# Two-layer decoder on one core: weights fetched one stage ahead, expert sends one to a step, routing in groups of two

## The reference, cut to what matters

```python
x = _layernorm(x + _L0_attn_ref(x, W_Q, b_Q, W_K, b_K, W_V, b_V, W_O, b_O))      # stage a
x = _layernorm(x + _L0_xattn_ref(x, ctx_1024, ...))                              # stage b
x = _layernorm(x + _L0_ffn_ref(x, router_w, e_bias, W_gate, W_up, W_down,
                               shared_gate, shared_up, shared_down))             # cd, m, cc
x = _layernorm(x + _L1_attn_ref(x, weight_qkv, weight_out))                      # stage d
x = _layernorm(x + _L1_xattn_ref(x, ctx_1024, Wq, Wk, Wv, Wo, gq, gk))           # stage e
x = _layernorm(x + _L1_ffn_ref(x, gate_w, gate_proj, up_proj, down_proj))        # r, n, fc
```

```python
G = jnp.einsum('ecd,edi->eci', Xp, W_gate); U = jnp.einsum('ecd,edi->eci', Xp, W_up)
Y = jnp.einsum('eci,eid->ecd', jax.nn.silu(G) * U, W_down)
out = jnp.zeros((T, d), x.dtype).at[slots_token].add(Yf)
shared = jax.nn.silu(x @ shared_gate.T) * (x @ shared_up.T) @ shared_down.T
```

## Time and profile before

| | us |
|---|---|
| median of 3 runs | 3529.71 (3528.15 to 3530.47) |
| the profiled execution | 3531.17 |
| its span | 3529.2 |

### The profile page before, as it was taken

How to read it: one execution, slowest core, us unless ns; L and a number is a source line. 1 busy time by engine, 2 the same in 40 slices (tenths; PEclk the granted TensorE clock), 3 DMA queues, 4 the chain that set the end, 5 groups by cost and what they waited for, 6 DMA issues and landing times. The chain is left out here.

```text
span 3529.2 us, 59019 instructions
## 1 busy us (share of the span) xinstructions
PE 3179.0 (90%) x21140; PEld 2651.9 (75%) x21140; DVE 2078.1 (59%) x3732; ACT 1277.4 (36%) x3276; POOL 1443.5 (41%) x1470
## 2 busy tenths in 40 slices
PE   6999999999969999799896999599999999759992
PEld 5887878878847777677685777488888888748881
DVE  4666566676646666421164777466666678335566
ACT  2333333333346666201102333244444444224340
POOL 3454343444322434300162222355555566344445
PEclk9999999999979999889898999799999999679996
DMA  4001016023210100349663111411101000156664
GB/s 167 20 17 50 0 35 229 0 93 114 90 68 29 54 26 20 143 137 343 195 151 104 37 44 35 144 35 32 35 23 35 12 23 12 55 206 220 220 222 155
DMA packets 138293, 320.20 MB, mean 91 GB/s; under 512 B 18473, under 2 KB 30505, under 8 KB 135586
## 3 DMA queue, kind: packets, MB, share of 16 engines
q1 hardware_dynamic: 121058, 280.90, 23.5%
q0 software_dynamic: 15360, 36.25, 3.9%
q10 hardware_dynamic: 1728, 1.07, 0.1%
HBM read 234.21 MB, written 98.04 MB: 94 GB/s over the span
## 5 line engine op out<-in xcount | busy, mean ns | idle before, releaser
L377 POOL TENSOR_TENSOR a_sq<-a_tq,a_sinq 128x256 f32<-128x256 f32 x128 | 149.8, 1190 | 355.6 <-DVE a_tq L448 355.6
L377 POOL TENSOR_TENSOR a_sk<-a_tk,a_sink 128x256 f32<-128x256 f32 x128 | 123.7, 985 | 90.0 <-DVE a_tk L448 90.0
L343 ACT COPY a_probT<-bank 128x512 f32<-128x512 f32 x64 | 37.5, 585 | 327.5 <-PE bank L653 327.5
L390 POOL TENSOR_TENSOR e_sk<-e_tk 128x512 f32<-128x512 f32 x64 | 66.7, 1042 | 210.3 <-DVE e_tk L475 210.3
L330 ACT ACTIVATE a_sm<-a_sm,a_nmax 128x128 f32<-128x128 f32 x256 | 99.8, 391 | 121.4 <-DVE a_nmax L535 121.4
L335 ACT ACTIVATE e_prob<-bank,e_nb,e_rq 128x128 f32<-128x128 f32 x256 | 113.7, 455 | 82.5 <-DVE e_nb L540 82.5
L881 ACT ACTIVATE b_prob<-bank,b_nb 128x128 f32<-128x128 f32 x512 | 139.0, 386 | 10.0 <-DVE b_nb L1077 10.0
L975 POOL TENSOR_TENSOR d_prob<-d_prob,d_nmax 128x1024 f32<-128x1024 f32 x32 | 64.0, 1999 | 181.7 <-DVE d_nmax L1072 181.7
L2203 POOL TENSOR_TENSOR n_wu_lo<-nw_wu,n_wu_hi 128x1408 fp32r<-128x1408 f32 x23 | 74.1, 3223 | 143.4 <-DVE n_wu_hi L2247 143.4
L470 DVE TENSOR_TENSOR a_kr<-a_kr,a_sk 128x512 f32<-128x512 f32 x64 | 66.4, 1038 | 88.9 <-POOL a_sk L377 88.9
L1074 DVE TENSOR_REDUCE b_nmax<-bank 128x8 f32<-128x1024 f32 x64 | 77.7, 1214 | 67.4 <-PE bank L1213 66.7
(11 more groups left out here) (507 smaller groups left out, 10669.1 us busy)
## 6 DMA issues: line engine op xcount, KB each, us to landing
packed<-all_zero SPq DMA_DIRECT2D x32, 1024.0 KB, 8.0
cw_wg<-in_c_wg SPq DMA_DIRECT2D x32, 512.0 KB
cw_wu<-in_c_wu SPq DMA_DIRECT2D x32, 512.0 KB
cw_wd<-in_c_wd SPq DMA_DIRECT2D x32, 512.0 KB
nw_wg<-in_f_wg SPq DMA_DIRECT2D x23, 704.0 KB
nw_wu<-in_f_wu SPq DMA_DIRECT2D x23, 704.0 KB
nw_wd<-in_f_wd SPq DMA_DIRECT2D x23, 512.0 KB
n_xe<-packed SPq DMA_DIRECT2D x46, 256.0 KB, 2.7
```

Of the source, the lines that this page charges most:

```text
L343: nc.scalar.copy(probT[:], pP[:, :]).then_inc(act_pt, 1)
L377: step = nc.gpsimd.tensor_tensor(o, i, s, ALU.mult)
L390: nc.gpsimd.tensor_tensor(sk[:], tk[:], tk[:], ALU.mult).then_inc(g_k, 1)
```

## The change

There are five edits.

1. One buffer `staged` of three parts holds the raw weights for all stages and lives as long as the kernel; `first_x` holds the first x tile of a stage. Stage a's first weights (q, k, v) and its first x tile are fetched in the opening block, behind the identity and before and after the two small constants. Each stage then fetches the next one's ahead: a fetches b's x tile and q, k, v, o (on SP, in the slot of group 3, batch 14, after a wait until its own weights have been split and all but its last stores have landed); b fetches the shared expert's three weights (on SP, before the last four stores), and cd and cc both use these, so both loads `part.load` go; cc fetches d's q, k and v (on ACT, each after the last use of the part it replaces); d fetches e's v, k, q (on SP). The first x tiles of d and e, and d's wo, are still loaded in their own stage. The load of the second x tile no longer waits for the first tile to be turned.
2. In `PLAN_8` the eight sends of a pair lie one to a step: four in steps 4 to 7 of the odd slot, four in steps 0 to 3 of the next even one. The last four of pair 5 go to the beginning of POOL's queue in cd. The pieces of the output move: ("o2", 8, 10) goes behind "p" in step 0, and the output of steps 6 and 7 is cut at 4, 6, 8.
3. The experts' buffers `xe` and `ye` of stage m lie in parts of `base` that are free then.
4. In cc the last batch adds its four gathered rows to x first, and the output of the shared expert last.
5. In r there are eight groups of two batches, each counted after the first batch of the next group. SP's queue in r ends with a wait for all sends and then the loads of stage n's first x tiles, which stood in stage n.

```diff
-            sp.dma_start(xin[:], x_src[0]).then_inc(x_in, 16)
+            if not head_ready:
+                head.fetch(sp)
+            sp.dma_start(xin[:], x_src[1]).then_inc(x_in, 16)
             context(0, 0)
-            for n in QK:
-                weights(n, 0)
             biases(0)
-            weights("v", 0)
-            sp.wait_ge(pe_x, done(0))
-            sp.dma_start(xin[:], x_src[1]).then_inc(x_in, 16)
             context(1, 1)
...
+                if ahead and g == G - 1 and is_batch(b, B - 2):
+                    for n in "kvo":
+                        sp.wait_ge(w_lo[n], rows_of[n] * G)
+                    if keep is None:
+                        sp.wait_ge(out_st, 16 * (B - 4))
+                    ahead(sp)
...
-            for n in KINDS:
-                sp.dma_start(raw[n][:], w_dram["w" + n]).then_inc(w_in[n], 16)
+            if "o" not in staged.raw:
+                sp.dma_start(raw["o"], w_dram["wo"]).then_inc(w_in["o"], 16)
             sp.dma_start(xres[:], x_src(0)).then_inc(r_in, 16)
...
+            if ahead:
+                for n in KINDS:
+                    sp.wait_ge(w_lo[n], 1)
+                ahead(sp)
             for b in range(B - 4, B):
...
-                    if isinstance(e, int) and b % 2 and b >= 5:
-                        router.send(pool, b // 2 - 2, e)
+                    if isinstance(e, int) and (b % 2, e >= 4) in ((1, False), (0, True)) and b >= 5:
+                        router.send(pool, (b - 1) // 2 - 2, e)
...
-        ["x", ("o2", 8, 10), "s", "p", ("o2", 10, 12)],
+        ["x", "s", "p", ("o2", 8, 12)],
...
-        ["s", "p", ("o", 0, 2), 1, ("o", 2, 5), 2],
-        ["p", ("o", 5, 7), 3, ("o", 7, 8), "pv"],
+        ["s", "p", ("o", 0, 2), 1, ("o", 2, 4), 2],
+        ["p", ("o", 4, 6), 3, ("o", 6, 8), "pv"],
...
-    "pool": [["c"], [], ["n"], ["q"], [0, 1], ["zl", "k", 2], [3, 4, 5], [6, 7]],
+    "pool": [["c", 4], [5], ["n", 6], ["q", 7], [0], ["zl", "k", 1], [2], [3]],
...
-            part.load(sp)
             prefetch(sp)
 
         @block.gpsimd
         def _(pool):
+            for n in range(router.K, 2 * router.K):
+                router.send(pool, LAST - 2, n)
...
-    GROUPS = ((0, 2), (2, 2), (4, 4), (8, 4), (12, 4))
+    GROUPS = [(b, 2) for b in range(0, B, 2)]
...
                 weights.load(sp, weights.number(sp, 0, w), w)
+            sp.wait_ge(sent, 16 * K * B)
+            for w in range(2):
+                weights.load_x(sp, packed.rearrange("(t r) d -> t r d", r=P), weights.place(sp, 0, w), w)
...
-                if g and b == GROUPS[g][0] + 1:
+                if g and b == GROUPS[g][0]:
                     count(g - 1)
...
+                for n, used in (("q", part.pe_g), ("k", part.pe_u), ("v", part.pe_o)):
+                    act.wait_ge(used, done(part.COUNT - 1))
+                    ahead(act, n)
...
-            if shared:
-                part.load(sp)
...
+                if shared_last:
+                    dve.wait_ge(part.pe_o, done(b - part.first))
+                    dve.wait_ge(v_k, done((K - 1) * b + K - 1))
+                    nc.vector.tensor_tensor(acc[:, n], part.pO[:, :], acc[:, n], ALU.add).then_inc(v_acc, 1)
...
                 sp.dma_start(ident[:], c["ident"]).then_inc(c_in, 16)
+                head_a.fetch(sp)
                 sp.dma_start(tri[:], c["tri"]).then_inc(c_in, 16)
                 sp.dma_start(ones[:], c["ones"]).then_inc(c_in, 16)
+                for n, source in first_of(of("a_")):
+                    staged_a.fetch(sp, n, source)
                 sp.wait_ge(g_z, 1)
                 sp.wait_ge(c_in, 48)
```

More of the change, by code:

```diff
@@ L782, in _ @@
             sp.sem_inc(out_st, 16)
-            sp.dma_start(xin[:], x_src(0)).then_inc(x_in, 16)
+            if not head_ready:
+                head.fetch(sp)
             if router:
@@ L1156, in turn_x @@
             def turn_x(b):
-                pe.wait_ge(x_in, landed(b))
+                first = isinstance(b, int) and b == 0
+                t = head.tile if first else xin
+                if first:
+                    pe.wait_ge(head.x_in, 16)
+                else:
+                    pe.wait_ge(x_in, landed(b - 1))
                 pe.wait_ge(act_v, done(b - 1))
                 for c in range(C):
-                    last = nc.tensor.transpose(pJ[:, P * c:P * c + P], xin[:, P * c:P * c + P], ident[:])
+                    last = nc.tensor.transpose(pJ[:, P * c:P * c + P], t[:, P * c:P * c + P], ident[:])
                 last.then_inc(pe_x, 1)
@@ L2112, in _ @@
         def _(sp):
-            def place(i, w):
-                return sp.value_load(weights.tile[0:1, bass.ds(2 * i + w, 1)], min_val=0, max_val=packed.shape[0] - 2)
-            def load_x(t, w):
-                for n in (2 * w, 2 * w + 1):
-                    sp.dma_start(xe[:, n, :], packed[t + n % 2]).then_inc(x_in[n], 16)
             def store(i, n):
@@ L2135, in refill @@
                     store(i, n)
-            for w in range(2):
-                load_x(place(0, w), w)
             with sp.Fori(0, ROUNDS - 1) as i:
@@ L2329, in _, with combine @@
             down(*LAST)
-def combine(nc, name, base, result, rows, weight, x_dst, K, shared=None):
+def combine(nc, name, base, result, rows, weight, x_dst, K, shared=None, ahead=None):
     R = 4
```

131 lines of the change are left out of this document (89 added, 42 removed).

## The result

The changed kernel takes 3497.01 us (median of 4 runs, 3493.3 to 3503.28); the kernel before, measured beside it, 3530.09 us (3528.15 to 3531.84). The ratio is 0.9908, with a 95% interval of 0.9891 to 0.9926: 33.1 us saved. The profiled execution has a span of 3497.9 us, 31.3 us less than before. The profile before says PE 3179.0 us busy; after, it is

A forecast was written before the change was run, and what follows sets the result against it. PE was busy 90% of the span, so gains lay in seams and stalls; -5 - 3 - 9 + 0 - 6 - 1 - 2 - 10 = -36 from 3531.17 us gave 3495.2 profiled, 3494 us median, range 3472 to 3514.

The forecast's parts named there:

- Stage b (-9): Stage b: spreading the sends removes ACT's kT stalls; 9 us of PE time saved, from -17 to +5.
- third rival: Stage b: GpSimd's queue sets the slots, each of 44 moved sends costs 1.27 us; +29, about 3559 us; chance 0.03.
- The seams a to b, cc to d, d to e (-3, -1, -2): Stage starts b, d, e: weights fetched ahead, so waits for wq go; 3, 1 and 2 us saved.
- r to n (-10): r into n: groups of two end sends sooner, x is loaded before the barrier; 10 us saved, from -4 to -15.
- cc (-6): Stage cc: 3 us of PE's gate-weight wait and 3 us of its creep go; range -3 to -12.
- first rival: Whole kernel: number of sends counts, not spacing; b 0, cc -3, r -6, sum -20, about 3510 us; chance 0.16.
- its sign for cc: Start of cc: the prediction is right if the first matmul comes within 1 us of the stage's start.
- a (-5): Opening of a: x, q, k, v issued sooner, v split earlier; scores start 2 to 8 us sooner, 5 taken.

The follow-up runs named there:

- c_after: The changed kernel unchanged, run again on the second group's chip: 3498.71 us, ratio 0.9905 to the kernel before.
- c_before: The kernel before, unchanged, run again with a trace on the second group's chip: 3530.83 us (one run).
- y_mix: Changed kernel with stage b's old plan and sends and n's first x loads back behind r's barrier: 3516.95 us, ratio 0.9953 to the kernel before.
- u1_sends: Changed kernel with stage b's plan and sends as before, on the first group's chip: 3480.12 us, ratio 0.9939 to the kernel before.
- x4_paced: Changed kernel with cc's gathers paced instead of 16 in a row, on the first group's chip: 3472.4 us, ratio 0.9923 to the kernel before.
- u3_staging: Changed kernel with all fetches ahead undone except stage a's, on the first group's chip: 3485.08 us, ratio 0.9957 to the kernel before.
- z_best2: Changed kernel with a's low part of v on DVE and at most two batches of cc's gathers in a row: 3491.62 us, ratio 0.9889.
- z_undo: Changed kernel with PE's old list in PLAN_8 and cc's old end, sends still spread: 3496.42 us (one run).
- u2_groups: Changed kernel with r's five old routing groups, on the first group's chip: 3479.73 us, ratio 0.9939 to the kernel before.
- y_best: Changed kernel with cc's gathers paced as in x4_paced and a's low part of v on DVE: 3495.13 us, ratio 0.9895 to the kernel before.
- c_after2: The changed kernel unchanged, control on the third group's chip: 3498.68 us, ratio 0.9917 to the kernel before.
- first pair: Traces of the kernel before and the changed kernel from the first measurement: medians 3530.09 and 3497.01 us.
- second pair: Later traces of both kernels unchanged, c_before and c_after: 3530.83 and 3498.71 us.
- first group's chip: Chip of u1_sends, u2_groups, u3_staging and x4_paced, whose traces show no stalls; the kernel before takes 3501.79 us there.

## Why the prediction was right, and where it wasn't

The forecast, 3494 us, was 3 us from the measured 3497, and the range held it. Term by term it is less even.

- **Stage b (-9): right in place and mechanism.** The waits "remote" are gone and odd slots are below 28 us, as the prediction asked; even ones are at 26.1, where it asked for 25.8. 9.5 and 12.3 us were measured, the term had 9. From the slot before the first send on it is 11.0 and 10.6 us (after: 1135.63 to 1444.72, before: 1140.89 to 1460.95; c_after: 1128.95 to 1439.23, c_before: 1142.57 to 1463.49), the rest lies ahead of the sends. y_mix shows that the spacing alone gives 12.0. The counting work of an odd slot, which the prediction put at 1.6 us, is 1.1 in u1_sends (27.0 against 25.9), so more of the old slots was stall than it reckoned. And a rest of the stall is left: PE waits 0.70 us for the matmul behind the third send of a row in c_after (L1218 in the odd slots) and 0.31 in x4_paced, and the odd slots take 27.4 and 27.0 us. The third rival (GpSimd sets the slots) didn't come: even slots grew by 0.27 us, not by a send each.
- **The seams a to b, cc to d, d to e (-3, -1, -2): right**, too small for the first. The table has 4.7 and 4.8 us where 3 was taken, and u3_staging 4.7 too. The part that was mis-sized is the context: its split was to come 0.4 us sooner and comes 2.6 sooner, counted from the stage's first DMA issue (985.30 less 980.29, against 989.83 less 982.26), and wq's split right behind it, as forecast.
- **r to n (-10): right.** 9.3 and 10.0. Two steps of it were off and made up for each other. The last send came only 7.5 us sooner, not 11, since eight sends and not four were still queued when the last target was ready at 3069.32. The table chain took 4.9 us and not the assumed 7.5. It isn't safe: in z_best2 and z_undo, with the same groups, it took 9.8 and 10.0, where nine sends and not four lay behind the last pause (the table of r above). The groups alone are worth 7.3 us on the chip without stalls.
- **cc (-6): wrong, by the whole term.** The failing step is the sentence that 3 us of the wait for the gate weights go and 3 more of the creep, since "two things load that stretch". The first did happen: the turn of x that waited comes 2.35 us after the start and not 5.16, and the first gate and up products are over 12.1 us after it and not 14.3. But neither PE's start nor its creep is last. In the kernel before, the same product ends at 1752.69 and DVE takes it at 1761.66, 9.0 us later:

```profile
1748.95 3.74 PE L1435 MATMUL bank<-cc_sxT,cc_wu 128*128 128x128 f32 x32
```

In the changed kernel it is 11.7 us (1732.82 to 1744.56), in u2_groups, without stalls, 0.1 (1719.67 to 1719.78). So DVE waits for a product that seems done, as ACT does in b, until the burst is through: the 16th gather is issued 19.7 us after the stage's start in both kernels, and the product is taken after 23.3 us before (1738.38 to 1761.66) and 23.8 after (1720.73 to 1744.56). What is won ahead of it is waited away. The creep that the prediction counted from windows of PE's busy time is in matmuls of the next batch, on which nothing waited yet. On the chip without stalls u3_staging and x4_paced differ by the 3 us of the first half of the term (16.0 and 12.9 us to the first product); the second half, the creep, doesn't exist there. The prediction had both facts in hand, the creep and the unchanged gathers, and didn't ask what is last for DVE. The first rival's "cc only -3" was nearer, for the same reason. And its sign for cc, the first matmul within 1 us of the stage's start, could not tell: it was at 0.5 us before the change too (1738.90).
- **a (-5): right at the scores** (-5.4 and -4.6), and in the end -2.0 and -7.2. Two things weren't in the sum. DVE's and GpSimd's low parts collided: 2.50 and 4.99 us before became 6.72 and 6.50. What that costs at the scores is 1.7 to 2 us by the controls of y_best and z_best2 (c_after, c_after2) and 0.4 to 1.2 by the other traces of the same chips (y_mix, z_undo), so its size is open. The Trainium skill, "GPSIMD Engine Reference", section "Specifications", says that GpSimd's SBUF interfaces are shared with VectorE and contended by VectorE's instructions with two SBUF inputs; both rows are such subtractions and agree. And in the first trace units after the scores ran at a lower clock, below.
- **The sum came out for a partly wrong reason.** In the first pair cc and a fell 5.8 and 3.0 us short, and the seam into b, b, cd and m gave 3.6 more; in the second pair a, the seam and b gave 7.3 more, which covers the missing 6.2 of cc. In d, e, n and fc, which the edits don't touch inside, single stretches are off by +3.8 and -4.5 us in the first pair, while their sum is -0.9 and +0.6.

The +3.8 in e is mostly the clock. The last output of e begins with the same wait in each kernel, 2.93 us for `e_z_lo`. Before, then after:

```profile
3027.73 0.50 PE L81 MATMUL bank<-e_wo_hi,e_z_lo 128*128 128x512 f32 x1 [2.93 <-DVE e_z_lo L503]
```

```profile
3007.93 0.79 PE L81 MATMUL bank<-e_wo_hi,e_z_lo 128*128 128x512 f32 x1 [2.93 <-DVE e_z_lo L505]
```

The matmuls behind it take 0.39 us each at 2.4 GHz (granted clock 1.00 from 3028 to 3030) in the one and 0.63 at 1.2 GHz (0.50 from 3008 to 3012) in the other, and from this matmul to the end of the stage it is 2.5 us more by that alone (8.64 against 6.17). In a, likewise, a window from 48 to 52 us has a granted clock of 0.59 after, and the one from 50 to 54 us before has 1.00. c_after shows the fast form of both. The two pairs of traces differ by 5.2 us in a and by 4.8 in e with the same two kernels, so a difference of this size in one stage of one pair tells nothing by itself.

What stays open: why the chips differ, and how much of it the stalls are. On the first group's chip the kernel before takes 3502 us, and no stall shows; in the three other measurements it takes 3529 to 3532, with stalls at the same places. The kernel before was not traced on the first group's chip; with the same code of b, from the slot before the first send on, y_mix takes 19.7 us longer than u1_sends, and c_after, with the sends spread, still 7.5 longer than x4_paced, of which the eight slots are 2.0. Part of the rest is the clock at the end of b (granted 0.67 and 1.00 in the slot from 52 us behind the last x load on). Only one chip without stalls was seen, and of the possible differences only the load of the DMA engines was compared, which is about equal. The -4.5 us in n and fc have no explanation either; the second pair doesn't show them. What in a burst stops the other engines, the traces don't show: the gaps have no releaser, and why DVE or ACT takes a product so long after the record of its last matmul isn't shown either. In b the spread sends also lie in other steps of the slot; a run with them together in those steps was not made, and it is the table of r that speaks for the length of the row and against the place. And a version of cc with short bursts and a long enough lead wasn't tried.

## What to carry to other kernels

When a wait at the start of a stage goes, ask which event was last for the first consumer, here DVE's first hidden product; if it is not the one removed, the gain is nothing. To find it, compare when the consumer starts with when its input was written: a busy share or a creeping engine beside it can belong to other work. Spread indirect DMAs of GpSimd where the order allows it, but keep their lead over the consumer: rows of at most three left 0.4 us of stall in each odd slot of b, a row of six 2 to 3, one of 16 some 11. On one chip long rows cost nothing, so such a gain should be measured on more than one. Before a split or a subtraction is moved to an earlier time, look at what the other of DVE and GpSimd does at that time.

## What the runs showed of the hardware that was not expected

- The same program differs by 27 to 30 us between chips (3501.79 against 3528.68 to 3532.28). Beside bursts of indirect DMAs the chips differ by 11 us at the start of cc, by 13 in eight slots of b with the old sends (y_mix and u1_sends), and by 5 to 8 in the table chain of r.
- On chips with stalls, a row of 16 gathers at 1.27 us each makes PE run one or two matmuls at a time with gaps of 0.4 to 1.8 us, from the tenth gather on in the changed kernel and from the twelfth in the kernel before, and DVE takes a finished product 9.0 to 11.7 us late, when the row is through. In b the stall appears after the third send. DVE's small operations in r are not slower with up to eight sends in a row and take twice as long and more behind nine or ten.
- Two subtractions with both inputs in SBUF, one on DVE and one on GpSimd, took 6.72 and 6.50 us beside each other, and 2.50 and 4.99 apart; in other traces of the same code DVE's took 5.8.
- A PE wait of 2.93 us at the end of e is followed by matmuls of 0.63 us, the 1.2 GHz level, in three of the thirteen traces (after, u2_groups, z_best2) and of 0.39 or 0.40 us, the 2.4 GHz level, in the others.
